# A hybrid block of linear attention, transformer layers and gated mixing on one core: the sources' exponents split on POOL, their placement copied by ACT, and another order of all steps

## The chip, the core and the metric

The kernel runs on one core of a Trainium2 chip. Its engines are named as in the profile: PE (matrix products and transposes, accumulating into eight PSUM banks psA0 to psA3 and psB0 to psB3), PEld (the loading of PE's weights, which overlaps PE), DVE (vector engine), ACT (activation engine), POOL (GpSimd) and SP (which issues all DMAs of this kernel). Each engine works through its own list of instructions in order, and the lists meet only at semaphores. The metric is the device time of one execution in microseconds, lower is better, as the median of several runs.

## What is computed

The reference applies four residual steps to `x` of shape (16, 256, 128): 16 batches of 256 tokens with 128 features.

```python
x = x + attn_a(layernorm(x))    # log-linear attention, 32 heads of 64, causal
x = x + ffn(layernorm(x))       # layer 0: softmax attention (16 heads of 8), mixture of 8 experts
x = x + attn_b(layernorm(x))    # "mix": nine gated, rolled copies of a projection
x = x + ffn(layernorm(x))       # layer 1: the same weights as layer 0
```

The part that the change touches is in the first step. Cut to what matters:

```python
dt  = softplus(dt + dt_bias)                   # (B, T, 32)
lam = softplus(L * dl)                         # one weight per level of a Fenwick tree
gc  = cumsum(-exp(A_log) * dt, axis=1)
decay  = exp(gc[t] - gc[s])  for s <= t
lam_ts = lam[t, level(t, s)]
att = (C @ B.T) * decay * lam_ts               # (32, 256, 256) per batch
y   = att @ (x * dt) + D * x
y   = rmsnorm(y * silu(z)) * norm_w @ out_proj + b
```

The kernel computes decay, level weight and `dt[s]` as one exponential: exp((log lam[t] + gc[t]) + (log dt[s] - gc[s])). The first bracket belongs to the target and its level, the second is the source's exponent. Both are fp32 values that go through PE as sums of three bf16 parts (first part, the rest's first part, and what is left); making these parts is called the split.

## The kernel before

One batch is cut into 303 steps ("hops"), and 16 batches go through them in a software pipeline. The text PERIOD (line 124 on) lists the hops of one turn of the pipeline in order. A word such as `smax1.0+4@0574` means: the step smax, of layer 1, part 0, done for the batch that entered 4 turns ago, using the PSUM banks 0, 5, 7 and 4 (0 to 3 are psA, 4 to 7 psB). `order()` unrolls it to all 16 batches in 21 turns, leaving out batches that don't exist. Each engine then walks the whole list and issues its own part of every hop, so the one list sets the order on every engine and also which bank each product goes to. Nothing is decided at run time. `bank(hop)` gives the tile, the bank and the number of its use; `filled[b]` is raised by PE when a bank holds a result, `drained[b]` by the engine that has read it, and PE waits for the drain before it writes that bank again. Because PE is in order, a bank that comes free late holds up everything that is listed on PE behind it.

`order()` also puts in the changes of ACT's function table: the hops silu, zact and mix need one set, and gates, wexp, exps and parts of tail and outp the other. Each change of set in the list is one table load on ACT (lines 903 and 905). The unrolled list of before has 127 loads in all.

The hops that matter here, with the lines of the profile:

- gates 0 to 6 make the exponents. Gates 5 (L1170, DVE) adds gc to the targets' exponents, gates 6 splits: POOL splits the targets' exponents (L1433 to L1439, 128x512 each), DVE computes and splits the sources' (L1176 to L1184, 128x64 each), and POOL then spreads the sources' parts over a wider tile with six copies (L1446), which raises `s_spread`.
- place: PE transposes that tile into a PSUM bank (L607), and DVE copies it to SBUF as `placed` (L1189, 128x1024 bf16).
- weigh, wexp, prod, own, sum, gated (eight units per batch): PE builds the exponents (L657, L665), ACT takes exp (L980), DVE multiplies with QK (L1228, 128x1024), POOL computes the diagonal term (L1515), PE multiplies with X (L678, L686), DVE multiplies with the gate Z (L1236).
- conv, tap, taps, silu, xt, xcopy and zgate, zact: the projections (L617) with their convolution (ACT L943, DVE six times L1201 and once L1211) and activations (ACT L955, L963), and the transposes of the result (L640).
- smax, rowmax, maxt: bounds of the attention scores. One smax fills four banks (L752), and the DVE empties each with one maximum (L1276). es, exps, ep: scores (L775, L776), their exp (ACT L1026), and the product with V (L790).
- tail 0 to 6 (in each layer): PE transposes the attention's result (L800), DVE normalises it (L1291, L1294), PE transposes back (L807, L808), ACT copies (L1031), PE multiplies with w_o (L814, L815), DVE adds the residual (L1302), then the layer norm (L1084 to L1091 on DVE, L1412 to L1401 on POOL), PE's transposes (L821, L822) and the router.
- up, relu, down, acc: the experts (PE L849, ACT L1049, PE L861, DVE L1357).
- mix: the gated rolls (PE L869 to L888, ACT L1068, DVE L1382, POOL L1499).

## Time and profile before

| | |
|---|---|
| time, median of 3 runs | 2222.94 us (2221.42 to 2224.94) |
| the profiled execution's own time | 2223.85 us |
| its span (first to last instruction) | 2222.1 us |
| mean granted PE clock | 0.961 of full speed |
| PE busy | 1985.2 us (89%), 16928 instructions |
| PE weight loads busy | 1492.8 us (67%) |
| DVE busy | 1801.5 us (81%) |
| ACT busy | 1512.9 us (68%) |
| POOL busy | 947.8 us (43%) |
| DMA queue q1 | 101.48 MB, 20.5% of 16 engines |

Busy time leaves out semaphore waits and idle time. The difference of 1.7 us between the profiled execution's time and its span lies around the span. In the middle of the run every turn of the pipeline repeats the same instructions, so one turn there (a period, some 125.7 us, bounded by two successive starts of the same instruction) stands for all of them. The turns at the start, where later steps have no batch yet, and at the end, where the first steps have none left, are the fill and the drain.

### The profile page before, as it was taken

To read this page: it belongs to the slowest core of one execution; us is meant where nothing else is said; L and a number is where in the kernel's file an instruction comes from. 1 tells how busy PE (TensorE), PEld (TensorE's weight loads), DVE (VectorE), ACT (ScalarE), POOL (GpSimd) and SP (SyncE) were. 2 spreads that over 40 slices of the span, in tenths; PEclk is the share of its full clock that TensorE was granted. 3 is DMA by queue.
4 is the path that set the end of the run, shared out by engine and by line. 5 is a ranking of instruction groups with operands and counts; after the bars stand their busy time and mean duration, and the time that the engine had idled before them with its cause. 6 is when DMAs were issued, how large, how long until landed. Compare 5 with 4: busy or idle time off the path is not lost. (4 is left out here: it accounts for less than half of the span.)

```text
span 2222.1 us, 48483 instructions
## 1 busy us (share of the span) xinstructions
PE 1985.2 (89%) x16928; PEld 1492.8 (67%) x16928; DVE 1801.5 (81%) x4399; ACT 1512.9 (68%) x3171; POOL 947.8 (43%) x1299
## 2 busy tenths in 40 slices
PE   3779989999999999999999999999999999996756
PEld 2556767676767777686777777676777767674534
DVE  6777888989898898989898898989899898754543
ACT  3566758778685868778686867868686867854323
POOL 5313353536344453626344453625444453533221
PEclk9889899999999999999999999999999999998777
DMA  5110122221203222220213222120213222121010
...
DMA packets 202306, 104.59 MB, mean 47 GB/s; under 512 B 126664, under 2 KB 188240, under 8 KB 196944
## 3 DMA queue, kind: packets, MB, share of 16 engines
q1 hardware_dynamic: 202064, 101.48, 20.5%
...
## 5 line engine op out<-in xcount | busy, mean ns | idle before, releaser
L1412 POOL TENSOR_SCALAR var_eps<-lnmv 128x2 f32<-128x2 f32 x128 | 41.5, 324 | 666.3 <-DVE lnmv L1087 665.0
L1228 DVE TENSOR_TENSOR att<-att,QK 128x1024 f32<-128x1024 f32 x192 | 283.2, 1502 | 6.0 <-ACT att L980 4.7
L1515 POOL TENSOR_TENSOR own<-X,ccoef 128x512 f32<-128x512 f32 x128 | 165.7, 1310 | 92.6 <-DVE ccoef L1220 32.5
L1276 DVE TENSOR_REDUCE nmax<-psB 128x2 f32<-128x512 f32 x304 | 193.4, 678 | 4.5 <-PE psB L752 3.4
L1201 DVE SCALAR_TENSOR_TENSOR work<-psA,c_conv_w,work 128x255 f32<-128x255 f32 (+2 forms) x405 | 181.7, 475 | 15.8 <-ACT work L943 15.6
L617 PE MATMUL psB<-xnT_a,c_w_in 128*128 128x256 f32 x576 | 177.0, 410 | 14.3 <-DVE work L1201 4.3
L1201 DVE SCALAR_TENSOR_TENSOR work<-psB,c_conv_w,work 128x255 f32<-128x255 f32 (+2 forms) x405 | 179.4, 474 | 1.1 <-ACT work L943 0.7
L1026 ACT ACTIVATE pt<-psA 128x512 f32<-128x512 f32 x288 | 162.5, 610 | 10.9 <-PE psA L776 10.8
L617 PE MATMUL psA<-xnT_a,c_w_in 128*128 128x256 f32 x512 | 155.7, 403 | 14.6 <-DVE hid L1201 7.8
L861 PE MATMUL psA<-c_w,hid 128*128 128x128 f32 x1152 | 161.6, 284 | 5.2 <-DVE nmax L1276 4.6
L988 ACT ACTIVATE att<-Z 128x1024 f32<-128x1024 f32 x64 | 62.4, 1046 | 151.0 <-DVE Z L1236 151.0
L861 PEld LDWEIGHTS psA<-c_w,hid 128*128 128x128 f32 x1152 | 147.3, 195 | 23.6 <-DVE nmax L1276 7.0
L1049 ACT ACTIVATE hid<-psB,c_b 128x256 f32<-128x256 f32 x249 | 117.2, 486 | 64.7 <-PE psB L849 64.7
L849 PE MATMUL psB<-x1T,c_w 128*128 128x256 f32 x512 | 156.1, 398 | 1.6 <-ACT qkf L1012 0.4
L849 PE MATMUL psA<-x1T,c_w 128*128 128x256 f32 x512 | 154.0, 393 | 0.2 <-ACT Z L963 0.2
L1276 DVE TENSOR_REDUCE nmax<-psA 128x2 f32<-128x512 f32 x208 | 136.9, 677 | 19.3 <-PE psA L752 19.3
L1499 POOL TENSOR_TENSOR O_sb<-O_sb,hid 128x256 f32<-128x256 f32 x128 | 97.7, 763 | 112.3 <-DVE hid L1382 106.5
L1357 DVE SCALAR_TENSOR_TENSOR ff<-psA,w_e,ff 128x128 f32<-128x128 f32 x288 | 86.6, 342 | 67.7 <-PE psA L861 67.2
L1026 ACT ACTIVATE pt<-psB 128x512 f32<-128x512 f32 x224 | 133.2, 619 | 8.5 <-PE psB L776 8.4
L617 PEld LDWEIGHTS psB<-xnT_a,c_w_in 128*128 128x128 f32 x576 | 102.3, 195 | 51.0 <-ACT Z L963 11.2
L1049 ACT ACTIVATE hid<-psA,c_b 128x256 f32<-128x256 f32 x247 | 114.2, 482 | 24.1 <-PE psA L849 16.8
L980 ACT ACTIVATE att<-psA 128x512 f32<-128x512 f32 x208 | 120.0, 606 | 10.2 <-PE psA L657 8.3
...
## 6 DMA issues: line engine op xcount, KB each, us to landing
qk_scr<-qparts SPq DMA_DIRECT2D x128, 192.0 KB, 3.8
...
q_max<-qk_scr SPq DMA_DIRECT2D x256, 32.0 KB, 1.9
k_max<-qk_scr SPq DMA_DIRECT2D x256, 32.0 KB, 1.8
...
low<-lvl_scr SPq DMA_DIRECT2D x256, 1.5 KB
...
```

Source lines behind the costliest of these rows:

```text
L617: e.matmul(t[:, 0:T], w_in[:, first + j * P:first + (j + 1) * P], xnT_a[:, :], start=True, stop=True).then_inc(filled[b], 1)
L849: e.matmul(t[:, 0:T], w_1[:, k, j * P:(j + 1) * P], x1T_b[lay][:, :], start=True, stop=True).then_inc(filled[b], 1)
L861: m = e.matmul(t[:, i * P:(i + 1) * P], hb[:, j, i * P:(i + 1) * P], w_2[:, 2 * k + j, :], start=(j == 0), stop=(j == 1))
L980: e.activation(att[:, :, c:c + 64], t[:, :].rearrange("p (t h) -> p h t", h=HG), ACT.Exp).then_inc(drained[b], 1)
L1026: e.activation(pt_b[a % PTS][:, :, :].rearrange("p h q -> p (h q)"), t[:, :], ACT.Exp, scale=float(AD) ** -0.5).then_inc(drained[b], 1)
L1049: e.activation(hid_b[lay][k % 2][:, j, :], t[:, 0:T], ACT.Relu, bias=b_1[:, 2 * k + j:2 * k + j + 1]).then_inc(drained[b], 1)
L1201: m = e.scalar_tensor_tensor(out=cv[:, back:], in0=t[:, 0:T - back], scalar=conv_w[:, c, tap:tap + 1], in1=cv[:, back:], op0=ALU.mult, op1 ...
L1228: e.tensor_tensor(att[:, :, :], att[:, :, :], bc(QK[:, kq, :], 1, HG), ALU.mult).then_inc(att_done, 1)
L1276: e.tensor_reduce(nmax[:, i, p0:p0 + 2], t[:, :].rearrange("p (h k) -> p h k", k=T), AX.X, ALU.max).then_inc(drained[b], 1)
L1357: m = e.scalar_tensor_tensor(out=ff[:, i, :], in0=t[:, i * P:(i + 1) * P], scalar=w_e[:, i, k:k + 1], in1=ff[:, i, :], op0=ALU.mult, op1=A ...
L1499: e.tensor_tensor(mix_acc[:, :], mix_acc[:, :], hid_b[0][j % 2][:, 1, :], ALU.add).then_inc(mix_sum, 1)
L1515: e.tensor_tensor(own_b[k % 2][:, :].rearrange("p (h c) -> p h c", c=HD), X[:, tt, h0 * HD:(h0 + HG) * HD].rearrange("p (h c) -> p h c", c ...
```

## The change

Three things change. First, the five DVE instructions that compute and split the sources' exponents in gates 6 are taken off DVE and issued by POOL, behind its own split of the targets' and ahead of the six spreading copies; the wait for `s_spread` of the batch before, which protected `gc`, moves to DVE's copy into `gc` in gates 4. Second, the copy of `placed` goes from DVE to ACT. Third, PERIOD is another list: the same 303 hops in another order, with other lags and banks. No other instruction is added or taken away, except that the unrolled list now has 99 table loads on ACT instead of 127.

```diff
@@ PERIOD, a few of its lines @@
-sum0.6+2@1 wexp0.7+2 acc1.5+5 smax1.0+4@0574 lvl0.0+1 sum0.7+2@6 smax1.1+4@1503 outp0.0+2@2 gated0.5+2 smax1.2+4@4560
+up1.5+4@06 relu1.6+4 tail0.2+2@7 down1.4+4@3 gated0.6+1 up1.6+4@42 down1.5+4@5 smax1.0+3@4127 tail0.3+2 sum0.7+1@0
-rowmax0.1+2 coef0.0+1 mix1.2+3@3 mix1.3+3@2 mix1.4+3@3 tail1.5+4@4 tail1.6+4 up1.0+4@25 mix1.5+3@6 mix1.6+3@3
+smax0.1+2@4723 mix1.1+3@51 tail1.4+4@4 rowmax0.0+2 rowmax0.1+2 mix1.2+3@0 bcp0.0+1 mix1.3+3@5 mix1.4+3@2 mix1.5+3@6
...
@@ ACT @@
+                elif what == "place":
+                    t, b, u = bank(hop)
+                    tb = t[:, :].bitcast(BF16)
+                    e.wait_ge(filled[b], u + 1)
+                    e.activation(placed[:, :, :, :].rearrange("p i k s -> p (i k s)"), tb[:, :], ACT.Copy).then_inc(drained[b], 1)
@@ DVE, gates 4 @@
                     t, b, u = bank(hop)
+                    if n:
+                        e.wait_ge(s_spread, n)
                     e.wait_ge(filled[b], u + 1)
@@ DVE, gates 6 and place @@
-                elif what == "gates" and k == 6:
-                    e.wait_ge(cl_ready, NT * (n + 1))
-                    if n:
-                        e.wait_ge(s_spread, n)
-                    e.wait_ge(dt_out, n + 1)
-                    e.tensor_tensor(gc[:, :, :], ln_dt[:, :, :], gc[:, :, :], ALU.subtract).then_inc(*own.step())
-                    e.wait_ge(*own.now())
-                    e.tensor_copy(s_parts[:, :, 0, :], gc[:, :, :]).then_inc(*own.step())
...
-                elif what == "place":
...
-                    e.tensor_copy(placed[:, :, :, :].rearrange("p i k s -> p (i k s)"), tb[:, :]).then_inc(drained[b], 1)
@@ POOL, gates 6, behind the targets' split @@
                     e.tensor_tensor(c_parts[:, :, 2, :], cr, c_parts[:, :, 1, :], ALU.subtract).then_inc(c_ready, 1)
+                    e.wait_ge(dt_out, n + 1)
+                    e.tensor_tensor(gc[:, :, :], ln_dt[:, :, :], gc[:, :, :], ALU.subtract).then_inc(*own.step())
+                    e.wait_ge(*own.now())
+                    e.tensor_copy(s_parts[:, :, 0, :], gc[:, :, :]).then_inc(*own.step())
+                    e.wait_ge(*own.now())
+                    e.tensor_tensor(gr[:, :, :], gc[:, :, :], s_parts[:, :, 0, :], ALU.subtract).then_inc(*own.step())
+                    e.wait_ge(*own.now())
+                    e.tensor_copy(s_parts[:, :, 1, :], gr[:, :, :]).then_inc(*own.step())
+                    e.wait_ge(*own.now())
+                    e.tensor_tensor(s_parts[:, :, 2, :], gr[:, :, :], s_parts[:, :, 1, :], ALU.subtract).then_inc(s_ready, 1)
```

**Place 1: the first layer's attention tail.** On DVE before, from the end of the sources' split to the residual of the first layer's attention (L1182 and L1184 are the split, L1291 and L1294 the tail's normalisation, L1302 the residual):

```order
L1182 CAST s_parts<-work 128x2x32
L1184 TENSOR_TENSOR s_parts<-work,s_parts 128x2x32
L1236 TENSOR_TENSOR Z<-psB,Z 128x4x128
L1291 RECIPROCAL rden<-psB 128x16
L1291 RECIPROCAL rden<-psA 128x16
L1294 TENSOR_TENSOR ff<-psB,rden 128x128
L1294 TENSOR_TENSOR ff<-psA,rden 128x128
L1228 TENSOR_TENSOR att<-att,QK 128x1024 x2
L1267 TENSOR_TENSOR V<-psA,c_bv 128x16x8 x2
L1228 TENSOR_TENSOR att<-att,QK 128x1024 x2
L1357 SCALAR_TENSOR_TENSOR ff<-psB,w_e,ff 128x128 x2
L1302 TENSOR_TENSOR x_0<-psB,src 128x256
```

The same stretch on DVE now (lines are those of the changed kernel: L1279 and L1282 are the normalisation, L1177 gates 5, L1216 the product with QK, L1290 the residual):

```order
L1224 TENSOR_TENSOR Z<-psB,Z 128x4x128
L1279 RECIPROCAL rden<-psA 128x16
L1279 RECIPROCAL rden<-psB 128x16
L1282 TENSOR_TENSOR ff<-psA,rden 128x128
L1282 TENSOR_TENSOR ff<-psB,rden 128x128
L1177 TENSOR_TENSOR work<-work,gc 128x256 x2
L1216 TENSOR_TENSOR att<-att,QK 128x1024 x2
L1290 TENSOR_TENSOR x_0<-psB,src 128x256
L1224 TENSOR_TENSOR Z<-psB,Z 128x4x128
L1089 BN_STATS lnst<-x_0 128x6 x2
L1091 BN_AGGR lnmv<-lnst 128x2
L1092 BN_AGGR lnmv<-lnst 128x2
```

The split is no longer ahead of the normalisation, gates 5 has come behind it, and one pair of products instead of two stands ahead of the residual.

On PE before, from behind the back-transposes of that tail to the second layer's first score bounds (L814 and L815 the product with w_o, L752 the bounds; their second bank, a psB, is the one that the product with w_o was in):

```order
L665 MATMUL psB<-low,low_sel 32x256 x2
L665 MATMUL psA<-low,low_sel 32x256 x2
L738 MATMUL psA<-c_Wv,srcT 128x128
L739 MATMUL psA<-c_Wv,srcT 128x128
L814 MATMUL psB<-c_Wo,attnT 128x128
L815 MATMUL psB<-c_Wo,attnT 128x128
L861 MATMUL psB<-c_w,hid_0 128x128 x4
L861 MATMUL psB<-c_w,hid_1 128x128 x4
L678 MATMUL psA<-c_ident,own 128x128 x4
L686 MATMUL psA<-att,X 64x128 x16
L752 MATMUL psA<-k_max,q_max 128x256
L752 MATMUL psB<-k_max,q_max 128x256 x3
```

The same stretch on PE now (the bank of w_o's product is the fourth that the bounds take):

```order
L807 MATMUL psA<-c_ident,ff 128x128
L808 MATMUL psA<-c_ident,ff 128x128
L849 MATMUL psA<-x1T,c_w 128x256
L849 MATMUL psB<-x1T,c_w 128x256
L814 MATMUL psB<-c_Wo,attnT 128x128
L815 MATMUL psB<-c_Wo,attnT 128x128
L861 MATMUL psA<-c_w,hid_0 128x128 x4
L849 MATMUL psB<-x1T,c_w 128x256
L849 MATMUL psA<-x1T,c_w 128x256
L861 MATMUL psB<-c_w,hid_1 128x128 x4
L752 MATMUL psB<-k_max,q_max 128x256
L752 MATMUL psA<-k_max,q_max 128x256 x2
```

One sum (L678, L686) and two down products stood between w_o's product and the bounds; now it is two down products and one up product.

**Place 2: gates 6.** On POOL before, from the targets' split on (L1433 to L1439), with the spreading copies and the next diagonal terms:

```order
L1433 CAST work<-work 128x2x256
L1435 TENSOR_TENSOR work<-work 128x2x256
L1437 CAST work<-work 128x2x256
L1439 TENSOR_TENSOR work<-work 128x2x256
L1446 COPY s_wide<-s_parts 128x4x24 x6
L1515 TENSOR_TENSOR own<-X,ccoef 128x512 x2
```

The same on POOL now (L1421 to L1427 the targets' split, L1429 to L1437 the sources', L1444 the spreading copies):

```order
L1513 TENSOR_TENSOR own<-X,ccoef 128x512 x3
L1421 CAST work<-work 128x2x256
L1423 TENSOR_TENSOR work<-work 128x2x256
L1425 CAST work<-work 128x2x256
L1427 TENSOR_TENSOR work<-work 128x2x256
L1429 TENSOR_TENSOR gc<-work,gc 128x64
L1431 CAST s_parts<-gc 128x2x32
L1433 TENSOR_TENSOR work<-gc,s_parts 128x64
L1435 CAST s_parts<-work 128x2x32
L1437 TENSOR_TENSOR s_parts<-work,s_parts 128x2x32
L1444 COPY s_wide<-s_parts 128x4x24 x6
```

Five instructions stand between the targets' split and the spreading copies, and the diagonal terms have moved ahead of the split.

**Place 3: the second layer's attention tail.** On DVE before, from the end of one convolution (L1211) over the residual (L1302) to the score bounds' maxima (L1276) and the normalisations (L1091) of mix's input `src` and of `x_1`:

```order
L1211 TENSOR_TENSOR work<-work,conv_edge 128x2x3
L1302 TENSOR_TENSOR x_1<-psB,src 128x256
L1084 BN_STATS lnst<-x 128x6 x2
L1086 BN_AGGR lnmv<-lnst 128x2
L1087 BN_AGGR lnmv<-lnst 128x2
L1084 BN_STATS lnst<-x_1 128x6 x2
L1086 BN_AGGR lnmv<-lnst 128x2
L1087 BN_AGGR lnmv<-lnst 128x2
L1276 TENSOR_REDUCE nmax<-psA 128x2
L1276 TENSOR_REDUCE nmax<-psB 128x2 x2
L1276 TENSOR_REDUCE nmax<-psA 128x2
L1091 SCALAR_TENSOR_TENSOR src<-x,lnmv,lnrs 128x128 x2
```

The same stretch on DVE now (L1092 ends the statistics of `x_1`, L1189 and L1199 are the convolution of another pair, L1096 the normalisations, L1264 the maxima):

```order
L1092 BN_AGGR lnmv<-lnst 128x2
L1189 SCALAR_TENSOR_TENSOR work<-psA,c_conv_w,work 128x255
L1189 SCALAR_TENSOR_TENSOR work<-psB,c_conv_w,work 128x255
L1189 SCALAR_TENSOR_TENSOR work<-psA,c_conv_w,work 128x254
L1189 SCALAR_TENSOR_TENSOR work<-psB,c_conv_w,work 128x254
L1189 SCALAR_TENSOR_TENSOR work<-psA,c_conv_w,work 128x253
L1189 SCALAR_TENSOR_TENSOR work<-psB,c_conv_w,work 128x253
L1199 TENSOR_TENSOR work<-work,conv_edge 128x2x3
L1096 SCALAR_TENSOR_TENSOR src<-x,lnmv,lnrs 128x128 x2
L1096 SCALAR_TENSOR_TENSOR x_1<-x_1,lnmv,lnrs 128x128 x2
L1264 TENSOR_REDUCE nmax<-psB 128x2
L1264 TENSOR_REDUCE nmax<-psA 128x2
```

A group of seven convolution instructions and both normalisations now stand between the statistics and the first maximum, and all eight maxima of the first two score bounds follow in one run.

On PE before, up to the transposes of `x_1` (L821, L822):

```order
L752 MATMUL psB<-k_max,q_max 128x256
L752 MATMUL psA<-k_max,q_max 128x256 x2
L752 MATMUL psB<-k_max,q_max 128x256 x2
L752 MATMUL psA<-k_max,q_max 128x256 x2
L752 MATMUL psB<-k_max,q_max 128x256
L617 MATMUL psB<-xnT_a,c_w_in 128x256
L617 MATMUL psA<-xnT_a,c_w_in 128x256
L869 MATMUL psB<-c_ident,src 128x128
L870 MATMUL psB<-c_ident,src 128x128
L875 MATMUL psB<-srcT,c_w_val 128x256
L821 MATMUL psB<-c_ident,x_1 128x128
L822 MATMUL psB<-c_ident,x_1 128x128
```

And now, where L821 writes the bank that the fifth of these maxima empties:

```order
L617 MATMUL psA<-xnT_a,c_w_in 128x256
L617 MATMUL psB<-xnT_a,c_w_in 128x256
L752 MATMUL psB<-k_max,q_max 128x256 x2
L752 MATMUL psA<-k_max,q_max 128x256 x2
L752 MATMUL psB<-k_max,q_max 128x256 x2
L752 MATMUL psA<-k_max,q_max 128x256 x2
L869 MATMUL psB<-c_ident,src 128x128
L870 MATMUL psB<-c_ident,src 128x128
L875 MATMUL psA<-srcT,c_w_val 128x256
L821 MATMUL psB<-c_ident,x_1 128x128
L822 MATMUL psB<-c_ident,x_1 128x128
L880 MATMUL psA<-srcT,c_w_mix 128x256
```

Before, those transposes took a bank that the second maximum of the first bound had emptied. In this stretch now each of the two score bounds follows directly on a projection (L617) whose two banks it takes over.

## Rows read from the trace of the kernel before

**Rows 1.** Windows; start:end, length, busy us (instructions) per engine, PEclk, DMA share, GB/s.
```profile
0.00:415.40 415.40, 335.81 (x2645) 246.25 (x2645) 324.39 (x746) 268.93 (x537) 164.13 (x209) 0.93 0.22 51
...
1299.10:1424.80 125.70, 119.39 (x1060) 90.81 (x1059) 112.11 (x272) 94.19 (x200) 58.30 (x81) 1.00 0.22 48
1803.70:2222.10 418.40, 330.38 (x2647) 242.61 (x2646) 243.28 (x661) 207.16 (x447) 142.01 (x211) 0.88 0.17 40
```

**Rows 2.** Timeline of PE in one period; start, length, engine, line, out<-in, [idle<-releaser].
```profile
1314.24 0.30 PE L807 MATMUL psB<-c_ident,ff 128*128 128x128 f32 x1 [0.67 <-DVE ff L1294]
...
1315.68 0.39 PE L814 MATMUL psB<-c_Wo,attnT 128*128 128x128 f32 x2
...
1316.13 1.95 PE L861 MATMUL psB<-c_w,hid 128*128 128x128 f32 x16
1317.91 0.60 PE L678 MATMUL psA<-c_ident,own 128*128 128x128 f32 x4
...
1321.89 0.28 PE L752 MATMUL psB<-k_max,q_max 32*128 32x256 bf16 x2 [1.27 <-DVE x L1302]
...
1386.19 0.67 PE L875 MATMUL psB<-srcT,c_w_val 128*128 128x256 f32 x2 [0.71 <-ACT srcT L1054]
...
1391.46 0.59 PE L849 MATMUL psA<-x1T,c_w 128*128 128x256 f32 x2
1391.89 0.59 PE L617 MATMUL psA<-xnT_a,c_w_in 128*128 128x256 f32 x2
...
1394.63 0.70 PE L880 MATMUL psB<-srcT,c_w_mix 128*128 128x256 f32 x2 [0.42 <-ACT hid L1049]
```

**Rows 3.** Timeline of DVE in the same period, around the sources' split.
```profile
1309.46 1.17 DVE L1178 CAST s_parts<-gc 128x64 bf16<-128x64 f32 x1
...
1312.59 0.22 DVE L1184 TENSOR_TENSOR s_parts<-work,s_parts 128x64 bf16<-128x64 f32 x1
...
1313.82 0.28 DVE L1294 TENSOR_TENSOR ff<-psA,rden 128x128 f32<-128x128 f32 x1
1314.19 4.13 DVE L1228 TENSOR_TENSOR att<-att,QK 128x1024 f32<-128x1024 f32 x2
...
1318.64 2.34 DVE L1228 TENSOR_TENSOR att<-att,QK 128x1024 f32<-128x1024 f32 x2
...
1321.43 0.41 DVE L1302 TENSOR_TENSOR x<-psB,src 128x256 f32<-128x256 f32 x1
```

**Rows 4.** Single lines; count, ns min/median/max, first and last start, shapes.
```profile
L1178 DVE CAST s_parts<-gc x16: 486/1174/1177, 25.8 to 1814.1; 128x64 bf16<-128x64 f32 x16
...
L1433 POOL CAST work<-work x16: 607/1607/1610, 25.5 to 1812.3; 128x512 bf16<-128x512 f32 x16
...
L1446 POOL COPY s_wide<-s_parts x96: 262/269/1314, 29.4 to 1818.6; 128x96 bf16<-128x96 bf16 x96
...
L1484 POOL TENSOR_TENSOR ff<-ff,c_before x32: 453/454/457, 221.0 to 2197.0; 128x128 f32<-128x128 f32 x32
```

**Rows 5.** Groups by shape on ACT and DVE; count | busy us, mean ns | idle before.
```profile
L905 ACT ACT_TABLE_LOAD x63 | 80.8, 1283 | 1.1
...
L963 ACT ACTIVATE Z<-psB,c_b_in 128x256 f32<-128x256 f32 x144 | 69.0, 485 | 14.5 <-PE psB L617 13.3
...
L922 ACT ACTIVATE s_wide<-Z 128x1024 bf16<-128x1024 f32 x1 | 1.0, 1040 | 0.0
...
L1189 DVE COPY placed<-psA 128x1024 bf16<-128x1024 bf16 x16 | 11.0, 689 | 1.2
```

**Rows 6.** Timeline of DVE in that period, second layer's attention tail.
```profile
1376.75 0.61 DVE L1091 SCALAR_TENSOR_TENSOR ff<-ff,lnmv,lnrs 128x128 f32<-128x128 f32 x2
1377.31 0.48 DVE L1201 SCALAR_TENSOR_TENSOR work<-psA,c_conv_w,work 128x255 f32<-128x255 f32 x1
...
1380.02 0.42 DVE L1302 TENSOR_TENSOR x<-psB,src 128x256 f32<-128x256 f32 x1
...
1381.68 0.66 DVE L1276 TENSOR_REDUCE nmax<-psA 128x2 f32<-128x512 f32 x1
```

65 lines of the change are left out of this document (28 added, 37 removed).

## The prediction

> **What bounds the kernel now.** I read the windows first [rows 1]. In one period of the middle PE is busy for 119.4 of 125.7 us at full clock (95%), DVE for 112.1 (89%), ACT for 94.2 and POOL for 58.3 (46%). PE's instructions are the same after the change, so in the middle the change can give back at most PE's idle time, 125.7 - 119.4 = 6.3 us a period, however much it takes off other engines. Fill and drain are different: in the first 415.4 us PE is idle for 79.6 us, in the last 418.4 for 88.0 and its granted clock is 0.88. They are chains of dependent steps with a DMA round trip in each attention.
>
> Then PE's timeline in one period [rows 2], to see what the 6.3 us are. The largest piece is 1.27 us before the second layer's first score bounds, whose second bank DVE's residual L1302 had still to read; 0.67 us precede the transposes L807, for DVE's L1294; 0.71 us precede the second product of mix, for ACT's copy of the transposes ahead of it, and 0.42 a gate of mix, for an activation. The other 3.2 us are smaller pieces.
>
> DVE's timeline tells why the first two arise [rows 3]. The sources' split runs from 1309.46 to 1312.81 and its casts take 1.17 us each; only then comes the normalisation, which ends at 1314.10, and PE's 0.67 us of waiting ends there. Behind it DVE has two pairs of products, 4.13 and 2.34 us, and reaches L1302 at 1321.43. So PE's two largest DVE waits stand behind the very work that the change removes.
>
> **The change part by part.** *The split leaves DVE.* From L1178 to the end of L1184 it takes 3.35 us of DVE's time [rows 3], with the subtraction ahead of it (another 0.6 at the most by its neighbours) 3.9 a period. The cast alone takes 0.486 us at its shortest and 1.174 as a rule, while POOL's cast of the targets takes 0.607 or 1.607 [rows 4]: they are issued together and hold each other up. The 0.67 us wait goes, since the normalisation is at least 3 us earlier against PE (place 1).
>
> *The residual and the score bounds.* In the new order PE needs, from the normalisation's end to the fourth bank of the bounds: the back-transposes 0.3, one up 0.87 (two starts 0.43 apart), w_o 0.45, a down 0.89, an up 0.87, a down 0.89 and three quarters of the bounds 0.25, together 4.5 us [rows 2]. DVE needs: gates 5, two additions, 2 x 0.41 taken as L1302's; one pair of products, 2.3 (the short pair) to 4.1 (the long one); L1302 itself 0.41; together 3.5 to 5.3 [rows 3]. So 0 to 0.8 us of wait are left of 1.27; I take 0.3, a gain of 1.0. With the 0.67 this is 1.6 us (0.9 to 1.9).
>
> *POOL takes the split.* POOL on 64 columns is not in the trace. From below, five instructions like the spreading copies, 0.27 each, 1.3 us; from above, three products of 128x128 at 0.454 and two casts held up as long as the targets' 1.607, 4.6 us [rows 4]. I take 1.8, nearest to the copies, since nothing on DVE is now issued together with it by design. Against it stands that POOL's first cast and the copies (0.269, at most 1.314) lose their partner in collision: some 1 us back. POOL is at 46%, and the parts are needed by place's transposes half a period later, so both ends cost nothing on PE in the middle. In the fill, for the first batch, 1 to 2 us more before the spreading copies lie beside the level tables' DMA round trip: nothing. The moved wait on `s_spread` is for an event almost a period old: nothing.
>
> *The collisions move.* The Trainium skill says (page "SBUF — State Buffer", section "SBUF: two separate sides") that DVE and GpSimd take a shared port pair as an exclusive lock for a whole instruction. The trace agrees with its 0.486 against 1.174 us. It speaks against this change as far as five more POOL instructions can now lock out products such as L1228; that is one of the rivals below, priced from rows.
>
> *The copy of placed* costs DVE 0.689 us and will cost ACT about as much as its own 128x1024 instruction to bf16 from SBUF, 1.040 [rows 5]; bounds 0.69 and 1.25. On DVE it stood right behind the second layer's normalisation. ACT is relieved at the same time: 28 of 127 table loads go, two of eight in a period, 2 x 1.283 = 2.57 us [rows 5]. Net ACT is 1.5 us a period shorter. Table loads stood in the mix stretch, ahead of the activation for which PE waited 0.42 us. Of the 3.2 us of small pieces and this 0.42, 3.6 together, every one stands at a place that is rearranged; some go and some come back elsewhere. I take 1.3 us off, a third, and add the new ones that I can see one by one.
>
> *New tight places* (place 3). First, behind the second layer's transposes only one projection (0.87 us) remains before L807; reciprocals and L1294 need some 0.9 us and two handovers: 0.3 us of wait. Second, each of the two score bounds follows a projection directly and takes over both of its banks; ACT empties it with an activation of 0.485 us [rows 5] that can't start before PE's end: 0.5 + 0.5 = 1.0. Third, L821 needs the bank of the fifth maximum. On DVE from the normalisation to that maximum: normalisation 0.56, seven convolution instructions 2.71, residual and two statistics 1.66, seven convolution instructions again 2.71, two normalisations 1.1, five maxima of 0.66, together 12.0 us [rows 6]. On PE in the same stretch: five projections at 0.87, transposes, w_o and place's transposes of about 0.45 each, two bounds of 0.3, mix's first two products 0.3 and 0.45, together 7.5, the waits of 1.0 just named and the old 0.71, and some 0.8 for the rest of the stretch: 10.0. So PE waits about 2.0 us at L821 (0 if DVE is ahead, 3.5 if collisions hold it).
>
> *The sum* in a period: -1.6 - 1.3 + 0.3 + 1.0 + 2.0 = +0.4, and not all of it adds up: a PE held for 2.0 us at L821 finds everything behind it ready, and the mix stretch, where the 0.42 and other small pieces stood, follows right there. I take 1.3 us more off for these, so -0.9 us a period, bounds -3.0 and +2.0. It counts 12.5 times: from 415.4 to 1803.7 us are 11 periods [rows 1], and I add 1.5 for the partial turns on both sides where both layers run. That is -11 us. Fill and drain: DVE's 3.9 + 0.7 us per batch stand on the path only while it leads in the fill, and the new lags lengthen or shorten no chain by more than some hundredths of a period: 0 +- 7 us. 2223.85 - 11 = 2213 for an execution like the profiled one, which lies 0.9 above the median: 2212.
>
> **The rivals.** *A, DVE's relief reaches PE everywhere.* DVE has 4.6 us a period less and ACT 1.5, and DVE arrives in place 3 early enough, so only the 0.3 and 1.0 remain as new, and another third of the 3.6 us of small pieces goes, since DVE is ahead: -1.6 - 1.3 + 1.3 - 1.2 = -2.8 a period, x 12.5 = -35: 2188. For it: both largest waits have DVE behind them [rows 2, 3]. Against: L821's bank depends on 12 us of DVE work in a fixed order, and DVE can't begin it before PE's own transposes.
>
> *B, the second layer's tail holds PE, slower than before.* If collisions with POOL (a pair of products took 4.13 us in one place and 2.34 in another [rows 3]) or the first convolution's activations put DVE later in place 3, PE waits 4 us instead of 2 at L821 and 0.5 more at mix's gates. Net +1.6 a period, +20: 2243. It decides from the point where the wait at L821 exceeds 3 us. For it: the count above already gives 2.0 without any collision. The rule of the Trainium skill cited above acts in this direction.
>
> *C, shifted.* New waits replace the old in size: 2223, within 3 us. For it: PE has only 6.3 us a period to give, and the ends of the estimate lie on both sides. Against: DVE and ACT both lose work.
>
> *D, the copy on ACT.* ACT's instruction is 1.04 us in a stretch where it empties eight projection banks; if it stands ahead of one that PE wants, +1 us a period. It is a part of B's and C's width.
>
> **How the numbers follow.** Forecast 0.40 (2212, its own range 2203 to 2221), A 0.16, B 0.25, C 0.19. What can't be told from no change is 0.2%, 4.4 us. Faster by more: most of the forecast (0.36), all of A and a little of C (0.04): 0.56. Within: 0.04 of the forecast, 0.12 of C and 0.01 of B: 0.17. Slower: 0.27. The range 2192 to 2241 leaves out half of A and a third of B.
>
> **What would show it.** L1178's successors on POOL well below 1 us each and no DVE work in gates 6; no wait of PE at the first layer's L807 and under 0.8 at the second layer's first bounds; a wait at the second layer's L821 of 1 to 3 us for a maximum, and two of about 0.5 for ACT's projections; PE idle 5.4 us a period. The forecast is wrong if the period is above 125.7 us (B, if the wait at L821 is above 3), below 123.5 (A), or if fill and drain together change by more than 7 us, which nothing here prices.

## The result, and the profile after

The changed kernel takes 2161.6 us (median of 4 runs, 2157.2 to 2165.2), the kernel before 2223.9 beside it (2221.4 to 2225.1): ratio 0.972, 95% interval 0.970 to 0.974. That is 62 us less where 11 were forecast; 2161.6 lies outside the range of 2192 to 2241. The profiled execution took 2165.2 us, its span is 2163.3.

The windows of after, cut at the same instructions as [rows 1] (start:end, length, busy us (instructions) per engine, PEclk, DMA share, GB/s); the second row is a period with a stretch at half clock, the third one without:

```profile
0.00:412.70 412.70, 329.96 (x2659) 247.62 (x2659) 310.31 (x724) 269.99 (x540) 167.73 (x231) 0.91 0.22 53
1143.90:1266.70 122.80, 118.15 (x1061) 92.04 (x1060) 107.89 (x267) 93.22 (x200) 59.64 (x86) 0.99 0.22 49
1267.30:1388.30 121.00, 116.84 (x1060) 90.47 (x1059) 106.79 (x267) 92.92 (x199) 59.13 (x86) 1.00 0.21 50
1751.50:2163.30 411.80, 322.50 (x2633) 242.70 (x2632) 238.10 (x654) 203.76 (x442) 135.99 (x214) 0.88 0.16 40
```

Against [rows 1]: the eleven middle periods take 1751.5 - 412.7 = 1338.8 us instead of 1388.3 (-49.5), the fill 412.7 instead of 415.4 (-2.7), the drain 411.8 instead of 418.4 (-6.6). A period takes 121.0 us instead of 125.7. DVE is busy 5.3 us less in it (4.6 forecast) and ACT 1.3 less (1.5 forecast), POOL 0.8 more. But look at PE: its instructions are the same (1060), the clock is 1.00 in both, and yet its *busy* time fell too, from 119.4 to 116.8 us. So its idle time went from 6.3 to 4.2, which is 2.15 us, and 2.55 us went that the profile doesn't show as idle. That second number is what this case is about.

PE's timeline at the three places of the prediction (start, length, engine, line, out<-in, count, [idle<-releaser]); the first two rows are the first layer's attention tail, the others the second layer's:

```profile
1281.62 0.33 PE L807 MATMUL psA<-c_ident,ff 128*128 128x128 f32 x1
...
1285.95 0.28 PE L752 MATMUL psB<-k_max,q_max 32*128 32x256 bf16 x1
...
1335.81 0.59 PE L617 MATMUL psA<-xnT_a,c_w_in 128*128 128x256 f32 x2
1336.86 0.30 PE L807 MATMUL psB<-c_ident,ff 128*128 128x128 f32 x1 [0.45 <-DVE ff L1282]
...
1337.54 0.60 PE L617 MATMUL psB<-xnT_a,c_w_in 128*128 128x256 f32 x2
1337.98 0.59 PE L617 MATMUL psA<-xnT_a,c_w_in 128*128 128x256 f32 x2
...
1342.75 0.59 PE L617 MATMUL psB<-xnT_a,c_w_in 128*128 128x256 f32 x2
1344.37 0.26 PE L752 MATMUL psB<-k_max,q_max 32*128 32x256 bf16 x1 [1.03 <-DVE work L1189]
...
1346.40 0.28 PE L752 MATMUL psB<-k_max,q_max 32*128 32x256 bf16 x2 [0.57 <-ACT Z L968]
...
1347.73 0.67 PE L875 MATMUL psA<-srcT,c_w_val 128*128 128x256 f32 x2 [0.56 <-ACT srcT L1059]
1348.59 0.33 PE L821 MATMUL psB<-c_ident,x 128*128 128x128 f32 x1 [0.19 <-DVE nmax L1264]
```

The two waits of [rows 2] that stood first, 0.67 us at L807 and 1.27 at L752, are gone in the first layer. In the stretch of the second layer's tail (place 3) there are new ones: 0.45 at L807, 1.03 and 0.57 at the two score bounds, 0.19 at L821.

DVE's timeline at the same places, to set beside [rows 3] and [rows 6]:

```profile
1279.71 0.28 DVE L1282 TENSOR_TENSOR ff<-psB,rden 128x128 f32<-128x128 f32 x1
...
1280.76 2.77 DVE L1216 TENSOR_TENSOR att<-att,QK 128x1024 f32<-128x1024 f32 x2
1283.48 0.43 DVE L1290 TENSOR_TENSOR x<-psB,src 128x256 f32<-128x256 f32 x1
...
1336.23 0.49 DVE L1282 TENSOR_TENSOR ff<-psA,rden 128x128 f32<-128x128 f32 x2
...
1347.86 1.28 DVE L1264 TENSOR_REDUCE nmax<-psB 128x2 f32<-128x512 f32 x2
```

In the first layer the residual (L1290 now) starts 3.5 us after the normalisation's end at 1279.99; before it was 7.3 us [rows 3], with two pairs of products between instead of one, and the split stood ahead of the normalisation besides. In the second layer DVE's chain from the normalisation's end at 1336.72 to the fifth maximum's at about 1348.5 is 11.8 us long; 12.0 were forecast from [rows 6].

POOL's timeline, first and last of the five instructions of the sources' split:

```profile
1286.42 0.32 POOL L1429 TENSOR_TENSOR gc<-work,gc 128x64 f32<-128x64 f32 x1
...
1287.80 0.31 POOL L1437 TENSOR_TENSOR s_parts<-work,s_parts 128x64 bf16<-128x64 f32 x1
```

From 1286.42 to 1288.11 that is 1.7 us (1.8 forecast). DVE isn't idle meanwhile: it works on results in PSUM banks, mostly the score bounds' maxima:

```profile
1286.65 0.68 DVE L1264 TENSOR_REDUCE nmax<-psB 128x2 f32<-128x512 f32 x1
```

The copy of the placement on ACT, by the groups (count | busy us, mean ns | idle before):

```profile
L953 ACT ACTIVATE placed<-psB 128x1024 bf16<-128x1024 bf16 x16 | 16.5, 1034 | 0.0
```

It was forecast at 1.04 us [rows 5].

PE's waits in the eleven middle periods, as far as they come in every period or nearly (us in total, times, longest):

```profile
PE psB L752 <- DVE work L1189: 14.3, 11, 1.3
PE psB L752 <- ACT Z L968: 6.2, 11, 0.6
PE psA L875 <- ACT srcT L1059: 6.2, 11, 0.6
PE psB L657 <- DVE nmax L1264: 5.3, 11, 0.5
PE psA L880 <- ACT hid L1073: 5.0, 11, 0.5
PE psA L726 <- DVE src L1096: 2.6, 10, 0.3
PE psB L821 <- DVE nmax L1264: 2.1, 11, 0.2
PE psB L807 <- DVE ff L1282: 2.0, 11, 0.5
PE psA L617 <- ACT Z L968: 1.8, 11, 0.2
```

Nine kinds of wait, each once a period; three rarer ones (six times, 2.0 us in all) are left out. In the kernel before, the same view has fourteen, and the two waits of [rows 2] that stood behind DVE are the first and the third of them:

```profile
PE psB L752 <- DVE x L1302: 13.9, 11, 1.3
...
PE psB L807 <- DVE ff L1294: 7.3, 11, 0.7
```

### The profile page after: what moved, and what is told of

It reads as the page before. It is cut to its first block, busy times and chain, and to the rows that moved or that the text cites. A ratio compares the mean times of both kernels' runs of the same rounds, so it can differ in the third digit from the quotient of the medians.

```text
span 2163.3 us, 48454 instructions
## 1 busy us (share of the span) xinstructions
PE 1943.5 (90%) x16928; PEld 1491.8 (69%) x16928; DVE 1724.7 (80%) x4303; ACT 1496.7 (69%) x3159; POOL 951.5 (44%) x1379
## 3 DMA queue, kind: packets, MB, share of 16 engines
q8 instruction: 137, 2.24, 0.5%
## 4 chain that ended last, share of the span: by engine, by line
PE 65%; DVE 19%; POOL 5%; ACT 4%; issue 4%; SPq 1%; DMA 1%; DVEq 0%; POOLq 0%; ACTq 0%
PE psB L861 6%; PE psA L711 6%; PE psB L686 6%; DVE work L1189 5%; PE psB L849 5%; PE psA L849 4%; DVE nmax L1264 4%; PE psA L790 3%; PE psA L861 3%; PE psA L617 3%; PE psA L686 3%; PE psB L790 2%; PE psB L678 2%; PE psB L617 2%; PE psB L775 1%
## 5 line engine op out<-in xcount | busy, mean ns | idle before, releaser
L1216 DVE TENSOR_TENSOR att<-att,QK 128x1024 f32<-128x1024 f32 x192 | 271.2, 1439 | 20.1 <-ACT att L985 18.6
L1189 DVE SCALAR_TENSOR_TENSOR work<-psA,c_conv_w,work 128x253 f32<-128x253 f32 (+2 forms) x495 | 222.7, 473 | 8.0 <-ACT work L943 7.0
L1264 DVE TENSOR_REDUCE nmax<-psB 128x2 f32<-128x512 f32 x288 | 189.4, 682 | 39.2 <-PE psB L752 38.8
L617 PE MATMUL psA<-xnT_a,c_w_in 128*128 128x256 f32 x640 | 193.1, 401 | 6.3 <-ACT Z L968 2.2
L861 PE MATMUL psB<-c_w,hid 128*128 128x128 f32 x1408 | 192.0, 280 | 0.8 <-DVE nmax L1264 0.8
L861 PEld LDWEIGHTS psB<-c_w,hid 128*128 128x128 f32 x1408 | 177.4, 194 | 12.0 <-issue 5.6
L849 PE MATMUL psB<-x1T,c_w 128*128 128x256 f32 x544 | 164.9, 402 | 3.8 <-DVE work L1189 1.9
L1189 DVE SCALAR_TENSOR_TENSOR work<-psB,c_conv_w,work 128x255 f32<-128x255 f32 (+2 forms) x315 | 149.2, 474 | 8.1 <-ACT work L943 7.8
L1345 DVE SCALAR_TENSOR_TENSOR ff<-psB,w_e,ff 128x128 f32<-128x128 f32 x352 | 106.5, 344 | 61.4 <-PE psB L861 58.3
L1264 DVE TENSOR_REDUCE nmax<-psA 128x2 f32<-128x512 f32 x224 | 147.4, 682 | 0.0
L617 PE MATMUL psB<-xnT_a,c_w_in 128*128 128x256 f32 x448 | 141.5, 399 | 1.6 <-ACT att L985 1.3
L849 PE MATMUL psA<-x1T,c_w 128*128 128x256 f32 x480 | 140.4, 396 | 2.1 <-DVE nmax L1264 2.1
L617 PEld LDWEIGHTS psA<-xnT_a,c_w_in 128*128 128x128 f32 x640 | 114.2, 197 | 37.6 <-issue 8.8
L985 ACT ACTIVATE att<-psB 128x512 f32<-128x512 f32 x208 | 120.1, 603 | 17.3 <-PE psB L657 12.9
L686 PE MATMUL psB<-att,X 128*64 128x128 f32 x2048 | 130.8, 278 | 0.0
L711 PE MATMUL psA<-c_w_out,Z 128*128 128x128 f32 x1024 | 124.9, 281 | 4.9 <-DVE c_w_out L1229 4.9
```

Of the source, the lines that this page charges most:

```text
L617: e.matmul(t[:, 0:T], w_in[:, first + j * P:first + (j + 1) * P], xnT_a[:, :], start=True, stop=True).then_inc(filled[b], 1)
L686: m = e.matmul(t[j * HD:(j + 1) * HD, f * P:(f + 1) * P], X[:, s, fc + j * HD:fc + (j + 1) * HD], att[:, 2 * f + j, :], start=False, stop= ...
L711: m = e.matmul(t[:, k * P:(k + 1) * P], Z[:, f, k * P:(k + 1) * P], w_out[:, f, :], start=(f == 0), stop=(f == NF - 1))
L849: e.matmul(t[:, 0:T], w_1[:, k, j * P:(j + 1) * P], x1T_b[lay][:, :], start=True, stop=True).then_inc(filled[b], 1)
L861: m = e.matmul(t[:, i * P:(i + 1) * P], hb[:, j, i * P:(i + 1) * P], w_2[:, 2 * k + j, :], start=(j == 0), stop=(j == 1))
L985: e.activation(att[:, :, c:c + 64], t[:, :].rearrange("p (t h) -> p h t", h=HG), ACT.Exp).then_inc(drained[b], 1)
```

## The experiments

The questions were which part brings the gain, the moved work or the new order, and where 2.55 us a period come from that no idle shows. "Old order" is the PERIOD text of the kernel before. All ratios are against the kernel before, run beside it on the same chip.

### The moves alone, in the old order

The changed kernel with the old list (cut; the first line is the changed kernel's):

```diff
 PERIOD = """
-load_x0.0+0 exps1.1+4 ep1.0+4@3 ...
+weigh0.6+2@2610 gated0.4+2 exps0.3+3 ...
```

> The kernel before with the two moves of work only (sources' split on POOL, placed copied by ACT), in the old order with its 127 table loads. Theory O (the order does it): the moves free PE only of the waits that stood behind the split on DVE, 0.67 us at L807 and 1.5 us at the second layer's first score bounds, with some 0.5 us of cost behind them: period 125.7 to about 123, time 2190 to 2198. Theory R (DVE's relief does it, in any order): period near 121.5, time 2165 to 2175. Theory T (fewer table loads on ACT): hardly any gain, 2215 or more.

Measured: 2234.5 us, ratio 1.0054 (1.0037 to 1.0071). Theories O and R missed. The time lies inside theory T's open bound (2215 or more), but T's reason, the table loads, is refuted further down. The waits at L807 and at the residual's bounds are gone as expected, but PE's waits are now led by another:

```profile
PE psA L678 <- POOL own L1513: 33.8, 11, 3.1
```

POOL's timeline there tells why:

```profile
691.20 1.30 POOL L1429 TENSOR_TENSOR gc<-work,gc 128x64 f32<-128x64 f32 x1
...
694.45 1.32 POOL L1437 TENSOR_TENSOR s_parts<-work,s_parts 128x64 bf16<-128x64 f32 x1
...
697.99 2.04 POOL L1513 TENSOR_TENSOR own<-X,ccoef 128x512 f32<-128x512 f32 x2
```

DVE's timeline beside it:

```profile
690.71 2.88 DVE L1216 TENSOR_TENSOR att<-att,QK 128x1024 f32<-128x1024 f32 x2
693.98 0.49 DVE L1255 TENSOR_TENSOR V<-psA,c_bv 128x128 f32<-128x128 f32 x2 [0.40 <-PE psA L739]
694.38 2.46 DVE L1216 TENSOR_TENSOR att<-att,QK 128x1024 f32<-128x1024 f32 x2
```

PE's L678 wants POOL's own term 6 (697.99), and in the old order POOL has gates 6 ahead of it: the targets' split, now the sources' split, and the spreading. The split takes 4.6 us here (691.20 to 695.77) and 1.7 in the changed kernel. The three of its five instructions that run beside DVE's products L1216, which read two tiles in SBUF, take 1.1 to 1.3 us; the two between (693.75 and 694.13), beside an idle DVE and beside L1255, which reads a PSUM bank, take 0.31 and 0.24. In the changed kernel all five take 0.24 to 0.32 beside maxima that read PSUM. The Trainium skill says that the port pair which DVE and GpSimd share is an exclusive lock for a whole instruction, and that a DVE instruction takes it in a two-port mode or with two inputs in SBUF (page "SBUF — State Buffer", section "SBUF: two separate sides"); these two traces agree, 1.30 beside L1216 against 0.32 us beside L1264 for the same L1429. So it matters not whether DVE works but at what. And the price at the upper end of my bounds (4.6) was real, in the order that I didn't price.

### The moves in the old order, with POOL's own terms ahead of gates 6

```diff
-down1.3+4@0 acc1.3+4 prod0.5+1 gates0.6+0 weigh0.5+1@1745 own0.6+1 ...
+down1.3+4@0 acc1.3+4 prod0.5+1 weigh0.5+1@1745 own0.6+1 ...
-... prod0.7+2 own0.7+2 acc1.4+5 ...
+... prod0.7+2 own0.7+2 gates0.6+1 acc1.4+5 ...
```

> The changed kernel's code in the old order (the run with the old order and the moves, 2234.5 us), but with POOL's own terms 6 and 7 put ahead of gates 6 on POOL (gates 6 goes into the next turn). That run waited 3.07 us a period for POOL at sum 6, because own term 6 stood behind the sources' split, the targets' split and the spreading. Theory P (the old order failed with the moves only because of that queue behind POOL's gates 6; with it gone the moves pay in the old order too): the wait at sum 6 is gone, DVE keeps its 5.1 us less work a period, the period falls from 126.3 to about 123, and the time is 2185 to 2200. Theory W (the old order has the wait at another place as soon as this one goes, since its DVE chains were laid round the old waits): sum 6's wait goes, another of 1 to 2 us comes, 2205 to 2235.

Measured: 2192.4 us, ratio 0.9856 (0.9842 to 0.9871). Theory P. The window of one of its periods, and the five largest of the twelve kinds of wait that PE regularly has in the middle:

```profile
656.30:780.00 123.70, 119.36 (x1060) 90.85 (x1058) 107.12 (x266) 95.12 (x202) 61.04 (x86) 1.00 0.21 49
```

```profile
PE psB L875 <- ACT srcT L1059: 7.8, 11, 0.7
PE psB L880 <- ACT hid L1054: 4.6, 11, 0.4
PE psA L790 <- ACT pt L1031: 4.0, 22, 0.2
PE psA L752 <- ACT Z L968: 3.5, 11, 0.3
PE psA L861 <- DVE nmax L1264: 3.4, 10, 0.3
```

The period is 123.7 us. Compared instruction by instruction with the period of before, PE's distances from start to start agree everywhere but at two places: 0.73 us come back at L807 (0.67 was shown as idle) and 1.28 at the residual's bounds (1.27 shown). That is the whole effect of the moves: -2.0 us a period, where 1.6 (0.9 to 1.9) were forecast for these two. In time it is 32 us of the 62 (2224.4 beside it).

Now read its window against the changed kernel's: 4.3 us of idle here and 4.2 there, so by the idle time the new order does nothing. But the period is 2.7 us shorter there, and that is the order's half of the gain.

### The new order alone, and with each move alone

The new PERIOD with the split on DVE (behind its gates 5) and the placement's copy on DVE; then each of the two on DVE by itself:

```diff
-                elif what == "place":            # ACT
-                    e.activation(placed..., ACT.Copy)
+                elif what == "place":            # DVE
+                    e.tensor_copy(placed..., ...)
...
-                    e.tensor_tensor(gc..., ln_dt..., gc..., ALU.subtract)...    # POOL, gates 6, and the other four
+                    e.tensor_tensor(gc..., ln_dt..., gc..., ALU.subtract)...    # DVE, behind gates 5, and the other four
```

> The new order with the work where it was: DVE splits the sources' exponents (right behind its gates 5, since the new list would block otherwise) and copies placed. Theory O: most of the gain stays, the split stands ahead of one pair of products and the residual, so up to 1.5 us a period comes back: 2165 to 2185. Theory R: the gain is gone, 2210 or more. Theory T: 2161 to 2170, since the table loads stay at 99.

> The changed kernel's order with the sources' split on DVE (right behind its gates 5) and the copy of the placement on ACT. The run with both on DVE took 2289.6, the changed kernel 2161.6. Theory S (the split is what the new order can't carry on DVE: five dependent small instructions, about 1.8 us, in the stretch in which PE waits for DVE's products, and exclusion against POOL): most of the 128 us comes back with the split alone, 2230 to 2290. Theory C (the copy is what matters, 1.2 us just ahead of the second layer's attention tail): 2165 to 2190.

> The changed kernel's order with the split on POOL and the copy of the placement on DVE. Theory C (the copy on DVE delays the tail of the second layer's attention and through it the first score bounds): 2230 to 2270, with the wait at the first score bounds grown by 1 to 2 us a period. Theory S: 2165 to 2190. If both this and the one with the split on DVE lie in the middle (2190 to 2230), the two add up.

Measured: 2289.6 us (ratio 1.030, 1.029 to 1.032), 2214.4 (0.9957, 0.9942 to 0.9972) and 2223.9 (1.0005, 0.9991 to 1.0019). The first is theory R's bound (2210 or more) and refutes O and T. Both single ones lie between their theories, in the middle in which the two add up: the split costs the new order 53 us, the copy 62, together 115 of the 128 that both cost. PE's waits in the three kernels, one fence each in that order:

```profile
PE psB L752 <- DVE work L1200: 32.3, 10, 3.2
```

```profile
PE psB L861 <- DVE Z L1235: 30.1, 11, 2.7
```

```profile
PE psB L752 <- DVE work L1189: 32.2, 10, 3.2
```

The split on DVE makes PE wait 2.7 us for a product (L1235) behind it; the copy on DVE makes the first score bound wait 3.2 instead of 1.3; with both on DVE both waits come (the other one 2.9). But the waits are less than half of what the copy costs. A period of the kernel with the copy on DVE:

```profile
1262.00:1387.70 125.70, 119.85 (x1060) 93.09 (x1059) 107.60 (x268) 92.22 (x197) 59.31 (x85) 0.96 0.21 48
```

PE idles 1.7 us more than in the changed kernel (5.85 against 4.16) and is busy 3.0 us longer with the same instructions, for its clock is at half (0.50) for 10.2 us of every middle period, beginning in this one at 1378.4, at the end of the wait of 3.2 us. The new order can't do without the moves: alone it is 3% slower. The moves don't need the new order, as the 2192.4 above shows, only POOL's own terms ahead of them.

### Fewer table loads, in the kernel before

The hops of mix behind the last gate don't ask for their table set any more; 99 loads instead of 127, as in the changed kernel.

```diff
-needed = ("silu_set" if what in SILU_SET else ...
+needed = ("silu_set" if what in SILU_SET and not (what == "mix" and step > NG + 1) else ...
```

> The kernel before, with the last two mix hops (copies only) no longer asking for the silu set: 99 table loads instead of 127, everything else as before. Theory T: ACT's 2.57 us a period reach PE, period below 124, time 2200 or less. Theories O and R: only the small waits in and behind the mix stretch can go (0.16 to 0.42 each), 0 to 1 us a period: 2211 to 2223.

Measured: 2224.0 us, ratio 1.0002 (0.9989 to 1.0014). Theory T is refuted; the time lies 1 us above the range of O and R, within the scatter. 28 loads of 1.283 us are worth nothing to this kernel. In the new order they weren't tried.

### Three changes to the waits of the second layer's tail

The changed kernel, with a projection ahead of the first bound; then also the maxima ahead of x's normalisation; then the value projection between the two bounds, with other banks (the first line is the changed kernel's):

```diff
-smax0.0+2@5160 zgate0.5+1@34 smax0.1+2@4723 mix1.1+3@51 tail1.4+4@4 rowmax0.0+2
+zgate0.5+1@34 smax0.0+2@5160 smax0.1+2@4723 mix1.1+3@51 tail1.4+4@4 rowmax0.0+2
+zgate0.5+1@34 smax0.0+2@5160 smax0.1+2@4723 mix1.1+3@51 rowmax0.0+2 tail1.4+4@4
+zgate0.5+1@34 smax0.0+2@5160 mix1.1+3@72 smax0.1+2@3451 tail1.4+4@6 rowmax0.0+2
```

> The changed kernel with one projection (zgate part 5) moved ahead of the first layer's first score bound instead of behind it. PE waited there 1.03 us for a bank that DVE's convolution empties, and 0.57 us at the second bound. Theory 'a wait of PE counts one to one': the 1.03 us becomes about 0.2, the second stays near 0.5: 0.6 to 1.1 us a period less, 2149 to 2155. Rival 'the wait moves on' (the next DVE result, the fifth maximum, then ends last): within 3 us of the changed kernel, with a wait of about 1 us at L821.

> The variant of the changed kernel with the first score bound behind the projection (2168.2 us, wait moved to the value projection for DVE's first maxima, 1.56 us a period) with the first four maxima on DVE ahead of the normalisation of x, which took 1.1 us. Theory M (the maxima are the end of the chain there, and nothing needs the normalised x sooner): the wait at the value projection falls by about 1 us, that at x's transpose grows by less, the best period is 120.0 to 120.6, the time 2148 to 2160. Theory N (x's transpose waits in its place for the normalisation, now behind 2.4 us of maxima): the best period is 121 to 122 and the time 2162 to 2180.

> The changed kernel with the value projection of the mixing put between the first two score bounds on PE, in banks of its own (7 and 2), and the second bound in banks 3, 4, 5, 1: PE works at the projection while DVE takes the first maxima. Theory M (in that stretch DVE's chain ends last: it works from 1336.0 to 1350.2 with no idle longer than 0.3 us, and PE's order round it matters only as far as DVE gets its work sooner): the best period stays within 0.5 us of 121.05 and the time within 2155 to 2168. Theory B (PE's waits there, 1.03, 0.57, 0.56 and 0.19 us, are of the banks' making, and go with them): the period falls by 1 to 2 us, 2138 to 2150.

Measured: 2168.2 us (ratio 0.9756, 0.9741 to 0.9770), 2189.7 (0.9844, 0.9827 to 0.9860) and 2155.4 (0.9693, 0.9672 to 0.9714). The waits of the first and of the second:

```profile
PE psB L869 <- DVE nmax L1264: 10.7, 11, 1.0
PE psB L821 <- DVE nmax L1264: 7.4, 11, 0.7
```

```profile
PE psB L821 <- POOL x L1389: 26.1, 11, 2.4
```

In the first the 1.03 us at the bounds became 1.0 at the next instruction that wants a maximum (L869), and 0.19 at L821 became 0.7: the best period is 121.05 us as before. PE was 1.8 us ahead at the projection and level again at L821. The wait moved on, as the rival had it, but both forecasts of the time missed: 2168.2 is 6.6 us above the changed kernel, with eight stretches at half clock in the middle instead of four (31 us instead of 14). In the second x's transpose waits 2.4 us, for x has to pass through POOL (L1389) behind the normalisation, which I hadn't counted: theory M is wrong, and N had the cause, but the period of 123.0 and the time lie above its ranges. In the third PE is 0.8 us ahead behind L821 and loses it in a wait of 0.8 at the next projection but one, for a bank that ACT (L1073) empties behind DVE's L1370, which follows the last maximum; the period is 121.05, as theory M had it. All three say that DVE's chain ends that stretch. The third's 2155.4 us against 2161.6 goes with the half-clock stretches (one in its middle, four in the changed kernel's), and the two intervals overlap, so it isn't shown to be faster.

### A longer chain, and a third bank

The multiplications of the second layer's attention output done twice; and, apart from it, weigh 2 in bank 1 instead of 4 (its wait of 0.46 us); the last is the bank and the projection of above together.

```diff
+                        e.wait_ge(dve_step, own.n - NT + 1 + qt if lay == 0 else own.n)
+                        if lay == 1:
+                            e.tensor_tensor(o_tok..., heads[qt]..., bc(rden...), ALU.mult).then_inc(*own.step())
+                            e.wait_ge(*own.now())
```

```diff
-relu1.1+4 xt0.5+1@1 mix1.12+3 ... weigh0.2+1@64 ... xcopy0.5+1 own0.0+1 ...
+relu1.1+4 xt0.5+1@1 xcopy0.5+1 mix1.12+3 ... weigh0.2+1@61 ... own0.0+1 ...
```

> The changed kernel with one thing made longer by a known amount: the two multiplications of the second layer's attention output (DVE, 128x128, 0.49 us each) are done twice, one behind the other, in the chain at the end of which PE waits (0.45 us at the transposes of the output, 1.03 at the first score bound, 0.57 at the second). About 0.9 to 1.1 us a period is added to DVE there. Theory H (a wait costs PE more than the idle that the timeline shows): the period (121.05 us) grows by more than PE's visible idle does, by 0.2 us or more, and PE's busy time grows with no instruction added to it. Theory V (visible idle is the whole of a wait): both grow by the same, within 0.1 us. Time by either: 12 or 13 periods of 0.9 to 1.1 us, 2172 to 2180, if no half-clock stretches come on top.

> The changed kernel with the third unit's weighting (weigh 2) in bank 1 in place of bank 4, which the score bounds of step 2 have just filled, so that it doesn't wait for DVE's maximum; the copy of the transposed inputs 5 comes 3 places sooner on ACT to free bank 1. PE waits 0.46 us a period there by the timeline, and its instruction there starts 1.37 us later than in its usual pitch. Theory H (the hidden part comes back too): the best period falls from 121.05 by 0.9 to 1.4 us, the time to 2144 to 2153. Theory V (only what shows comes back): by 0.3 to 0.5, 2155 to 2159. Theory M (the wait moves on to the next bounds, whose bank 6 is drained no sooner): within 2 us of 2161.6.

> Both of the two edits before in one kernel. If they are independent, its gain over the changed kernel is the sum of theirs (by theories H and B together 2 to 3.4 us a period, 2122 to 2136; by V and M together 2150 to 2162). It is also the try at a kernel that beats the changed one.

Measured: 2162.2 us (ratio 0.9724, 0.9706 to 0.9743), 2159.6 (0.9715, 0.9695 to 0.9736) and 2159.5 (0.9709, 0.9688 to 0.9730): none differs from the changed kernel by more than the intervals. The last is what V and M add up to (2150 to 2162), not H and B.

The longer chain was a miss: the wait at L807 grew from 2.0 to 10.1 us in the eleven middle periods, the one at the bounds shrank from 14.3 to 9.2, and the period grew by only 0.25 to 121.3, not by 0.9 or more. Of the 0.25 some 0.07 shows as idle and 0.18 lies in PE's busy time, just short of H's 0.2. It doesn't tell H from V, for slack behind the place took up most of what was added.

The third bank does tell something. The stretch of PE from weigh 2 to the next up-projection in the changed kernel and in this one:

```profile
1365.35 0.39 PE L657 MATMUL psB<-high,placed 64*128 64x512 bf16 x1 [0.47 <-DVE nmax L1264]
...
1365.94 0.70 PE L849 MATMUL psA<-x1T,c_w 128*128 128x256 f32 x2
```

```profile
1357.74 0.29 PE L665 MATMUL psB<-low,low_sel 125*32 125x256 bf16 x2
...
1358.87 1.30 PE L849 MATMUL psA<-x1T,c_w 128*128 128x256 f32 x4 [0.83 <-DVE nmax L1264]
```

The wait at L657 is gone, and the up-projection (L849), which waited for nothing, now waits 0.83 us for the next maximum. It starts at the same time of the period in both, 99.0 us behind gates 4. So the same instructions, from the same start to the same end, show 0.47 us of idle in one kernel and 0.83 in the other. The missing 0.36 are in PE's busy time. So a wait can hide a part, as theory H has it, but H's times are missed: the gain went to the next wait (theory M, within 2 us).

## Why the prediction was wrong

**Step by step.** By what the timelines show as idle, the sum can be gone through term by term, in us a period:

| term | forecast | measured |
|---|---|---|
| L807 and the residual's bounds, first layer | -1.6 | -1.94 |
| smaller pieces and those that follow | -1.3 - 1.3 | -2.45 |
| L807, second layer | +0.3 | +0.45 |
| score bounds and L821, second layer's tail | +1.0 + 2.0 | +1.03 + 0.57 + 0.19 |
| shown idle, sum | -0.9 | -2.15 |
| not shown as idle | 0 | -2.55 |
| period | -0.9 | -4.7 |

The measured smaller pieces are what is left of the 2.15 when the other rows are taken off; all rows are of a period without half clock. That they came out near the forecast's -2.6 is luck: it took them off by thirds, without a count.

**The step that failed** is that every wait was priced at the idle that the profile shows, and what a wait costs beside it was put at nothing. It stands at the start of the prediction: "in the middle the change can give back at most PE's idle time, 125.7 - 119.4 = 6.3 us a period". The gain of 4.7 stayed below that, but 2.55 of it aren't idle time at all: forecast 0, measured -2.55, the largest error in the table. The rows of after show how it comes. In PE's timeline the pair at 1337.54 takes 0.60 us, but the next pair starts 0.44 later; the pair at 1335.81 also takes 0.59, its successor starts at 1336.86, and only 0.45 of that counts as idle. Without the wait it would have started at 1336.25: the wait cost 0.61, of which 0.16 is hidden in the busy time of the last matmul. Where the next matmul has another tile shape less is hidden: 1342.75 to 1344.37 is 1.62 us, and such a sequence (128x256, 128x256, then 32x256) takes 0.22 + 0.31 without a wait, so this one cost 1.09 and shows 1.03. In a stream the next instruction overlaps the last one's end. The Trainium skill says the same of the engine (page "TensorE: Matmul & The Clock Gate", section "Step-by-step: what each phase is for": one matmul's drain overlaps the next one's fill), and that PE's busy share is no good measure of how near a kernel is to its limit, since matmuls are pipelined (page "Perfetto Trace Analysis", section "Identifying the Most-Contended Engine"); the rows agree, and I had weighed neither.

From this the order's gain: the old order (the run with POOL's own terms ahead) and the new have the same idle, 4.3 and 4.2 us, but the old one has it in 17 pieces in a period (the twelve kinds of its list, one of them twice, and some below the 0.15 us from which the view lists a wait), the new one in 9; the kernel before has 19. Busy time is 119.1 to 119.4 us in a period of each of the three kernels in the old order, whether they idle 4.3 us or 7.2, and 116.8 in the changed kernel. In its variants it is much the same, 117.05 where PE idles 3.95 us (the projection between the bounds) and, with the split on DVE, where it idles 6.8:

```profile
903.00:1027.00 124.00, 117.16 (x1060) 90.41 (x1059) 109.78 (x273) 92.87 (x198) 58.17 (x80) 1.00 0.21 49
```

So it goes with the order and the number of pieces, not with how long PE waits. The starts in the traces let it be added up. For each matmul behind a piece of idle take the distance from the start of the one before it, less the idle shown, less the mean distance at which the same two shapes follow each other where no idle stands between. What is left is the hidden part (the profile models the ends of PE's instructions; the starts and the periods don't depend on that): 0.15 to 0.16 us behind a matmul whose successor has the same tile shape, 0.07 where the shape changes, 0.26 to 0.38 between matmuls that otherwise start together. A full period at full clock, from a start to the same start, has in us:

| kernel | pieces | idle | hidden | busy less hidden |
|---|---|---|---|---|
| before | 19 | 6.3 | 3.5 | 115.95 |
| moves, own terms ahead, old order | 17 | 4.4 | 3.2 | 116.2 |
| changed | 9 | 4.1 | 1.15 | 115.8 |
| changed, split on DVE | 10 | 6.8 | 1.3 | 115.9 |

Two pieces of each kernel at most stand between shapes that never follow each other without idle and aren't in the column. So 2.35 of the 2.5 us of busy time that went stood hidden at pieces of idle, and 2.0 of 2.45 against the other kernel in the old order. The rest, 0.2 to 0.4, can be of another kind, by an estimate of 4 x 0.09 us: PE changes the shape of its tile four times less in a period of the new order, and a matmul of 128x128 that follows one of 128x128 starts 0.11 us behind it, but 0.20 if the next has 128x64. That the tiling's mode can't change without a drain is what the Trainium skill has (page "TensorEngine Tiling (Array Packing)", section "Key Properties"); the traces agree with 0.09 us for it.

This sum says where the time was; it doesn't promise that a piece taken away gives its hidden part back. Of the two pieces that the moves removed in the old order 0.07 us came back beyond the idle, not 0.3, and where one wait alone was taken away, as weigh 2's, it moved to the next. Which single changes of the list took the eight pieces away stays open.

**The second miss** was L821: 2.0 us forecast, 0.19 measured. The chain on DVE was right (11.8 us for 12.0). But PE's own work between was 9.2 us where I had counted 8.3: six projections stand in the new list there and I took five, and the terms that I named add up to 7.05, not 7.5. And DVE's lateness showed earlier, at the first bound, whose bank wasn't emptied by ACT, as I had it, but by the convolution of part 7 on DVE (1.03). The whole place came out at 2.24 us where the forecast had 3.3, and the error of 1.06 adds to that of the hidden part in the same direction.

**The rivals.** A (DVE's relief reaches PE everywhere) had the sign, and by the forecast's own sign (a period below 123.5) it is A that came; its -2.8 a period stands against -2.15 of shown idle, with 2.24 us of new waits in place 3 where it had 1.3, and it too put the hidden part at nothing. B needed 3 us at L821. Either half by itself took more time than before (2234.5 for the moves in the old order, 2289.6 for the new order with the old work), but by other waits than B's. D didn't come: the copy takes 1.03 us and no wait names it. Table loads, which I used as a reason for small pieces going, were worth nothing (2224.0).

**The count of periods.** 11 x 4.7 = 51.7 against the 49.5 of the middle; most of the difference is half clock, of which before has three stretches of 3.4 us in the middle (periods of 127.4 us) and after four (122.8, the second row of the first fence): 1.7 us each. Fill and drain changed by -2.7 and -6.6, together -9.3, which is more than the 7 that the prediction named as a sign of being wrong. But it counted 1.5 periods of the gain there; at the measured 4.7 these are 7.1, and 2.2 remain for its own term of 0 +- 7. With the middle it is the span's 58.8.
